# Graph attention over a dense adjacency on one core: the last group of rows is projected beside the first chunk's products

## The chip, the cores and the metric

The kernel runs on one core of a Trainium2 chip. The metric is the device time of one execution in microseconds (us), the median of several runs. Engines: TensorE (PE; PEld its weight loads), VectorE (DVE), ScalarE (ACT), GpSimd (POOL), SyncE (SP, which only issues DMAs here). ACT issues DMAs too.

## The reference, cut to what matters

x is 4096 x 128 float32, adj 4096 x 4096 int32 of zeros and ones (67 MB), W 128 x 128, a 256 x 1.

```python
h = jnp.maximum(_layernorm(x, axis=-1), 0.0)
Wh = h @ W
a1, a2 = (a[:Fout, 0], a[Fout:, 0])
e = (Wh @ a1)[:, None] + (Wh @ a2)[None, :]
e = jnp.where(e > 0, e, ALPHA * e)          # ALPHA = 0.2
e = jnp.where(adj > 0, e, MASK_VAL)
attention = jax.nn.softmax(e, axis=1)
h_prime = attention @ Wh
out = x + jax.nn.elu(h_prime)
```

## The kernel before, in words

**Tiling.** The 4096 output rows are cut into four chunks of 1024 (c = 0 to 3), the 4096 columns of adj into eight units of 512 (u = 0 to 7), each of four tiles of 128 (q = 0 to 3). x is cut into eight blocks b of 512 rows, two of which make a group g of 1024 rows.

**The weights.** The weight of an entry factors: up to a factor per output row it is the larger of two exponentials, one of the output row (g_row, spread over the partitions) and one of the column (gq_word). VectorE makes the words of one tile (c, u, q) in one instruction, L826: max(g_row, gq_word) times the transposed adjacency byte, 128 x 1024. A word is 32 bits that hold the two float16 halves (high and low) of a weight. TensorE multiplies them with the values (Wh times the column's exponential, also as a high and a low float16, `val`): three matmuls of 128x129 for each of eight row tiles, 24 for one product (L1052 to L1054), summed in three PSUM banks `acc[:, 0:3]` over the whole chunk. The fourth bank, `aux`, is free for other things.

**The adjacency.** SP (from load 12 on SP and ACT, half each) loads it as int32 into a ring of four 2 MB slots `raw`. The list LOADS gives the order: an entry is a whole unit (two halves by rows, rows of 2 KB), half the rows of two units (rows of 4 KB), or a quarter of four units for a "set". A slot is asked for again when ACT has made bytes of it (`act_bytes`). ACT turns each half slot to bytes with a Sign of 128x2048 (`to_bytes`, `one_of_two_to_bytes`, `set_to_bytes`; L540, L552, L574). The bytes of a unit are transposed by TensorE (`turn`, 16 transposes, L1028) into `mask_t`, for the last four units of chunks 2 and 3 (the sets) by VectorE (`turn_set`, L806). `words` has four buffers, so VectorE runs up to four products ahead of TensorE (`words_free`).

**The start.** For each group g: VectorE takes statistics (`row_halves`, L741) and moments; ACT and POOL centre the rows (`centre`, L512, L418); TensorE transposes them (`turn_x`, L996) into `mask_t[:, 1]`; ACT rectifies them into `h_t` (L520); TensorE projects them (`project`, L1007) into banks 0 to 2 of acc; VectorE scales them into `wh_sb` (`keep_projected`, L767); ACT takes the exponentials (L528); VectorE makes the column words (`make_words`, `split_weights_sums`, L773 to L786); `spread_words` on TensorE and `row_copy` on ACT make g_row (L1016, L592, L596). Values: the product in float32 (`first_values` on VectorE for group 0, `weigh` L429 on POOL), the cast to float16 on ACT (`high_values`, L535), the rest on VectorE or POOL (`first_low_values` L797, L432). Before the change all four groups are projected before the first product, since they pass through the banks that the products sum into; POOL weighs groups 1 to 3 beside the first units.

**Order.** Each engine's program is written out by hand, in order; semaphores join them. Chunk 0 is special: units' turns, spreads of groups 1 to 3 (units 3 to 5) and the mean of Wh for `seed_row` (unit 6) stand between products. POOL, after its values, sums Wh for the mean; the tails of the chunks (division, elu, residual) run on DVE, POOL and ACT beside later products.

## Time and profile before

| | |
|---|---|
| median of 3 runs | 236.33 us (235.15 to 236.42) |
| profiled execution | 236.24 us, its span 234.5 us |
| PE busy | 219.9 us (94%) |
| DVE busy | 198.9 us (85%) |
| ACT busy | 158.3 us (68%) |
| POOL busy | 81.1 us (35%) |
| mean granted TensorE clock | 0.984 |
| HBM read | 70.32 MB |

Busy time is the union of an engine's instructions, so it says how long an engine had something to do, not that it did it at its peak. The timeline merges neighbouring instructions of one line; its bracket is the idle time of the engine ahead of the row and what ended it. The chain is followed back from the last instruction, at each step to what released it.

### The profile page before, as it was taken

The numbers are of one execution on the slowest core, as the hardware profiler recorded it, in microseconds if no ns is written. First come the engines' busy times: TensorE is split into PE (matmuls) and PEld (weight loads), VectorE is DVE, ScalarE is ACT, GpSimd is POOL, SyncE is SP. The second block draws the span as 40 slices with busy tenths as digits, with TensorE's granted clock in tenths as the row PEclk, the third lists the DMA queues.
The fourth block names the chain that finished last, engine by engine and source line by source line (L and its number), as shares of the span: only waits on it lengthen the run. The fifth ranks groups of instructions, "written<-read, shape, count | busy, mean of one in ns | idle before, by whom it ended". The sixth has DMA issues, their size and how long they took to land.

```text
span 234.5 us, 8071 instructions
## 1 busy us (share of the span) xinstructions
PE 219.9 (94%) x3608; PEld 213.9 (91%) x3608; DVE 198.9 (85%) x266; ACT 158.3 (68%) x139; POOL 81.1 (35%) x68
## 2 busy tenths in 40 slices
PE   5969999999999999999999999999997899999980
PEld 1659899999999999999999999999997899999980
DVE  3999988765687997877787987899999999998766
ACT  3598899997786689874666666686569630991043
POOL 3648118789100031999300200000008900089000
PEclk9997999999999999999999999999999999999996
DMA  6999999999999999999999999999999930402002
GB/s 216 345 392 404 407 408 408 407 408 407 407 408 407 409 402 410 411 402 404 247 319 352 343 325 338 355 365 328 307 405 409 395 120 0 182 3 89 6 0 91
DMA packets 25526, 72.93 MB, mean 311 GB/s; under 512 B 1554, under 2 KB 2068, under 8 KB 25492
## 3 DMA queue, kind: packets, MB, share of 16 engines
q1 hardware_dynamic: 17040, 49.81, 57.3%
q10 hardware_dynamic: 8452, 22.61, 27.0%
q8 instruction: 28, 0.46, 0.9%
q14 instruction: 6, 0.05, 0.1%
HBM read 70.32 MB, written 2.10 MB: 309 GB/s over the span
## 4 chain that ended last, share of the span: by engine, by line
PE 59%; DMA 10%; ACT 10%; DVE 9%; issue 7%; ACTq 4%; DVEq 0%
PE acc L1052 16%; PE acc L1054 16%; PE acc L1053 16%; DMA raw<-in_adj_dram 8%; PE mask_t L1028 8%; ACTq L585 4%; ACT second L574 3%; DVE words L826 2%; ACT mask L552 2%; DVE stats L741 1%; DMA first<-in_x_dram 1%; PE acc L1016 1%; DVE mask_t L806 1%; ACT neg L705 1%; ACT g_row L574 1%
## 5 line engine op out<-in xcount | busy, mean ns | idle before, releaser
L826 DVE SCALAR_TENSOR_TENSOR words<-g_row,gq_word,mask_t 128x1024 f32<-128x1024 f32 x96 | 119.7, 1276 | 25.1 <-PE mask_t L1028 11.9
L1052 PE MATMUL acc<-val,words 128*128 128x129 f16 x744 | 127.9, 220 | 0.3 <-DVE wh_sb L767 0.3
L1054 PE MATMUL acc<-val,words 128*128 128x129 f16 x744 | 127.9, 220 | 0.0
L1053 PE MATMUL acc<-val,words 128*128 128x129 f16 x744 | 127.9, 220 | 0.0
L552 ACT ACTIVATE mask<-raw,step_bias 128x2048 uint8<-128x2048 int32 x44 | 86.0, 1995 | 28.9 <-PE mask_t L1028 14.0
L1052 PEld LDWEIGHTS acc<-val,words 128*128 128x128 f16 x744 | 72.8, 98 | 0.5 <-issue 0.5
L1053 PEld LDWEIGHTS acc<-val,words 128*128 128x128 f16 x744 | 72.8, 98 | 0.1
L1054 PEld LDWEIGHTS acc<-val,words 128*128 128x128 f16 x744 | 72.8, 98 | 0.0
L1052 PE MATMUL acc<-first,words 128*128 128x129 f16 x256 | 44.0, 220 | 2.3 <-DVE words L826 1.5
L1053 PE MATMUL acc<-first,words 128*128 128x129 f16 x256 | 44.0, 220 | 0.0
L1054 PE MATMUL acc<-first,words 128*128 128x129 f16 x256 | 44.0, 220 | 0.0
L826 DVE SCALAR_TENSOR_TENSOR words<-g_row,first,mask_t 128x1024 f32<-128x1024 f32 x32 | 38.7, 1266 | 0.0
L462 POOL TENSOR_SCALAR hp<-hp 128x1024 f32<-128x1024 f32 x3 | 10.9, 3636 | 68.8 <-ACT neg L665 68.8
L1052 PEld LDWEIGHTS acc<-first,words 128*128 128x128 f16 x256 | 25.0, 98 | 3.1 <-DVE words L826 3.0
L1028 PE MATMUL mask_t<-ident_b,mask 128*128 128x128 bf16 x384 | 26.2, 223 | 0.0
L1053 PEld LDWEIGHTS acc<-first,words 128*128 128x128 f16 x256 | 25.1, 98 | 0.0
L1054 PEld LDWEIGHTS acc<-first,words 128*128 128x128 f16 x256 | 25.1, 98 | 0.0
L1028 PEld LDWEIGHTS mask_t<-ident_b,mask 128*128 128x128 bf16 x384 | 23.4, 100 | 0.1
L574 ACT ACTIVATE second<-raw,step_bias 128x2048 uint8<-128x2048 int32 x8 | 15.6, 1996 | 7.6 <-issue 7.6
L458 POOL TENSOR_TENSOR hp<-num,rz 128x1024 f32<-128x1024 f32 x3 | 5.7, 1897 | 42.3 <-DVE rz L837 42.2
L574 ACT ACTIVATE g_row<-raw,step_bias 128x2048 uint8<-128x2048 int32 x4 | 8.0, 2004 | 8.5 <-DMA raw<-in_adj_dram 6.9
L485 POOL COPY first<-val 32x640 uint32<-32x640 uint32 x16 | 11.4, 715 | 1.0
(113 smaller groups left out, 214.9 us busy)
## 6 DMA issues: line engine op xcount, KB each, us to landing
raw<-in_adj_dram SPq DMA_DIRECT2D x36, 1024.0 KB, 15.6
raw<-in_adj_dram ACTq DMA_DIRECT2D x12, 1024.0 KB, 11.6
raw<-in_adj_dram SPq DMA_DIRECT2D x16, 512.0 KB, 11.1
raw<-in_adj_dram ACTq DMA_DIRECT2D x16, 512.0 KB, 13.5
first<-in_x_dram SPq DMA_DIRECT2D x8, 256.0 KB, 6.8
val<-in_x_dram SPq DMA_DIRECT2D x2, 512.0 KB, 15.8
out_dram<-first ACTq DMA_DIRECT2D x2, 512.0 KB, 4.6
out_dram<-val ACTq DMA_DIRECT2D x1, 512.0 KB, 3.8
```

The costliest lines, as they stand in the source:

```text
L458: nc.gpsimd.tensor_tensor(hp[:], num[:, :, 0:F], rz[:].unsqueeze(2).broadcast_to([P, CT, F]), ALU.mult).then_inc(hp_ready, 1)
L462: nc.gpsimd.tensor_scalar(hp[:], hp[:], 0.0, -1.0, ALU.max, ALU.add).then_inc(pos_ready, 1)
L485: nc.gpsimd.tensor_copy(val_set_u[k * QUARTER:(k + 1) * QUARTER, 4 * m:4 * m + 4], val_u[m * QUARTER:(m + 1) * QUARTER, (4 + k) * BT:(5 + ...
L552: nc.scalar.activation(mask[:, mask_slot(c, u), h * BT:(h + 1) * BT], raw_two[at % RING][:, :, i * BLOCK:(i + 1) * BLOCK], ACT.Sign, scale ...
L574: nc.scalar.activation(pair_bytes[PAIRS[c][k]][:, :, h], raw[:, at % RING, :, k * 256:(k + 1) * 256].rearrange("p t (m x) -> p m t x", m=2 ...
L585: act.dma_start(raw[k * QUARTER:(k + 1) * QUARTER, at % RING], adj_set[c, 1, h, k]).then_inc(set_in[at % RING], 16)
L705: last = nc.scalar.activation(neg[:, t], num[:, t, 0:F], ACT.Exp, scale=rz[:, t:t + 1])
L826: nc.vector.scalar_tensor_tensor(words[:, q], g_row[:, c * CHUNK:(c + 1) * CHUNK], word, bytes_t, ALU.max, ALU.mult).then_inc(words_ready, 1)
L1028: last = nc.tensor.transpose(maskt_pairs[:, i % 2, h, t * P:(t + 1) * P], mask_pairs[:, mask_slot(c, u), t, :, h], ident_b[:])
L1052: nc.tensor.matmul(acc_tile(t), high, v[:, 0, 0:V], start=first and t % PT == 0, stop=False, skip_group_check=True)
L1053: nc.tensor.matmul(acc_tile(t), high, v[:, 1, 0:V], start=False, stop=False, skip_group_check=True)
L1054: last = nc.tensor.matmul(acc_tile(t), low, v[:, 0, 0:V], start=False, stop=False, skip_group_check=True)
```

## The change

Group 3's transposes, projection, constants, values and g_row leave the start and go between products of chunk 0 (g_row into chunk 1), through the fourth bank `aux`. TensorE turns unit 0 before it transposes x 4 and 5, and begins with the products when group 2 is kept. VectorE's statistics of blocks 6 and 7 go into units 1 and 2, their moments to (2, 3), behind a new wait for the low values of group 2; its keeps of group 3 go into unit 5, the constants are made for groups 1 and 2 at (1, 1) and for group 3 at (5, 3). Values 1 (the second half of group 0) go from VectorE to POOL. Units 2 and 3 of chunk 0 are loaded and made to bytes as whole units (rows of 2 KB); unit 1 is loaded before x 6 and 7. The row copies on ACT move accordingly, those of group 3 to loads 14 and 16 of chunk 1, and VectorE's seed_row to the end of chunk 0.

The diff; left out are hunks that only move counts of semaphores:

```diff
@@ -51,7 +51,7 @@
-    LOADS = [(0, u, None) for u in range(2)] + [(0, (u, u + 1), k) for u in (2, 4, 6) for k in range(2)]
+    LOADS = [(0, u, None) for u in range(4)] + [(0, (u, u + 1), k) for u in (4, 6) for k in range(2)]
     LOADS += [(1, (u, u + 1), k) for u in (0, 2, 4, 6) for k in range(2)] + [(SETS, (u, u + 1), k) for u in (0, 2) for k in range(2)]
@@ -346,9 +346,11 @@
             load_raw(0, 1)
+            load_raw(1, 0)
+            load_raw(1, 1)
             for b in range(6, NB):
                 load_x(b)
-            for at in range(1, C * U):
+            for at in range(2, C * U):
@@ -418,9 +420,22 @@
+            def first_values(k):
+                tt = slice(k * BT, (k + 1) * BT)
+                pool.wait_ge(z_ready, 1)
+                nc.gpsimd.tensor_tensor(v32[:, 0, tt], wh_sb[:, tt, 0:F], dv[:, tt].unsqueeze(2).broadcast_to([P, BT, F]), ALU.mult
+                                        ).then_inc(v32_first, 1)
+            def first_low_values(k):
+                tt = slice(k * BT, (k + 1) * BT)
+                pool.wait_ge(vh_ready, k + 1)
+                pool.wait_ge(vl_first, k)
+                nc.gpsimd.tensor_tensor(val[:, tt, 1, 0:F], v32[:, 0, tt], val[:, tt, 0, 0:F], ALU.subtract).then_inc(vl_first, 1)
             def weigh(g):
-                pool.wait_ge(z_ready, 2)
+                pool.wait_ge(z_ready, 2 if g < 3 else 3)
@@ -434,12 +449,20 @@
             inverse_deviation(1, BT, CT)
-            for g in range(1, G):
+            def centre_group(g):
                 centre(2 * g)
                 inverse_deviation(g + 1, g * CT, (g + 1) * CT)
-            for g in range(1, G):
-                weigh(g)
+            centre_group(1)
+            first_values(1)
+            centre_group(2)
+            first_low_values(1)
+            weigh(1)
+            weigh(2)
+            centre_group(3)
+            weigh(3)
...
@@ -517,7 +540,7 @@
                     act.wait_ge(wh_ps, 3 * (b // 2 - 2) + 3)
-                nc.scalar.activation(h_t[:, b % 4], turned_bank(b), ACT.Relu, scale=-1.0).then_inc(ht_ready, 1)
+                nc.scalar.activation(h_t[:, b % 4], turned_bank(b) if b < 6 else aux, ACT.Relu, scale=-1.0).then_inc(ht_ready, 1)
@@ -629,36 +652,41 @@
             high_values(0, BT, CT)
+            to_bytes(0, 1, 0)
+            to_bytes(0, 1, 1)
+            exponentials(1, 3)
+            to_bytes(0, 2, 0)
+            to_bytes(0, 2, 1)
+            high_values(1, 0, CT)
+            to_bytes(0, 3, 0)
+            to_bytes(0, 3, 1)
+            high_values(2, 0, CT)
+            two_to_bytes(4)
             centre(6)
             centre(7)
-            to_bytes(0, 1, 0)
+            one_of_two_to_bytes(5, 0)
             rectify(6)
+            one_of_two_to_bytes(5, 1)
             rectify(7)
-            to_bytes(0, 1, 1)
-            exponentials(1, G)
-            two_to_bytes(2)
-            two_to_bytes(3)
-            high_values(1, 0, CT)
-            two_to_bytes(4)
-            high_values(2, 0, CT)
-            two_to_bytes(5)
+            two_to_bytes(6)
+            one_of_two_to_bytes(7, 0)
+            exponentials(3, G)
+            one_of_two_to_bytes(7, 1)
+            row_copy(1, 0)
             high_values(3, 0, CT)
-            row_copy(1, 0)
-            two_to_bytes(6)
+            one_of_two_to_bytes(8, 0)
             row_copy(1, 1)
-            one_of_two_to_bytes(7, 0)
-            row_copy(2, 0)
-            one_of_two_to_bytes(7, 1)
-            row_copy(2, 1)
-            one_of_two_to_bytes(8, 0)
-            row_copy(3, 0)
             one_of_two_to_bytes(8, 1)
             one_of_two_to_bytes(9, 0)
-            row_copy(3, 1)
+            row_copy(2, 0)
             one_of_two_to_bytes(9, 1)
             load_half(9 + RING)
+            one_of_two_to_bytes(10, 0)
+            row_copy(2, 1)
+            one_of_two_to_bytes(10, 1)
+            load_half(10 + RING)
@@ -674,8 +702,11 @@
-            for at in range(U + 2, C * U):
+            for at in range(U + 3, C * U):
                 c, u, h = LOADS[at]
+                if at in (14, 16):
+                    row_copy(3, (at - 14) // 2)
                 if u is None:
@@ -764,7 +795,7 @@
                 dve.wait_ge(rstd_ready, g + 2 if g else 1 + (t1 > BT))
-                nc.vector.tensor_tensor(wh_sb[:, tt], projected(acc[:, k, :], t1 - t0),
+                nc.vector.tensor_tensor(wh_sb[:, tt], projected(acc[:, k, :] if g < 3 else aux, t1 - t0),
                                         half_rstd[:, tt].unsqueeze(2).broadcast_to([P, t1 - t0, W2]), ALU.mult).then_inc(wh_ready, 1)
...
@@ -855,33 +886,38 @@
             first_low_values(0)
-            first_values(1)
             for k in range(3):
                 keep_projected(1, k)
-            row_halves(6)
-            link(row_halves(7))
-            moments(4, 3 * CT, 4 * CT)
-            first_low_values(1)
-            for k in range(3):
-                keep_projected(2, k)
             dve.wait_ge(grow_ready, 2)
             for k in range(3):
-                keep_projected(3, k)
+                keep_projected(2, k)
             weights(0, 0, 2)
             weights(0, 0, 3)
             for u in range(1, U):
                 for q in range(BT):
-                    if (u, q) == (1, 2):
-                        make_words(1, G, 6)
-                        split_weights_sums(1, G, 6)
-                        dve.wait_ge(word_ready, 4)
-                    if (u, q) == (7, 2):
-                        dve.wait_ge(mean_ps, 1)
-                        dve.wait_ge(consts, 6)
-                        nc.vector.tensor_scalar(seed_row[:, 0:F], aux[:, 0:F], SEED / N, None, ALU.mult).then_inc(mean_ready, 1)
+                    if (u, q) == (1, 1):
+                        make_words(1, 3, 6)
+                        split_weights_sums(1, 3, 6)
+                    if (u, q) == (1, 3):
+                        row_halves(6)
+                    if (u, q) == (2, 1):
+                        link(row_halves(7))
+                    if (u, q) == (2, 3):
+                        dve.wait_ge(vl_ready, 2)
+                        moments(4, 3 * CT, 4 * CT)
+                    if u == 5 and q < 3:
+                        keep_projected(3, q)
+                    if (u, q) == (5, 3):
+                        make_words(3, G, 9)
+                        split_weights_sums(3, G, 9)
                     weights(0, u, q)
+            dve.wait_ge(mean_ps, 1)
+            dve.wait_ge(consts, 6)
+            nc.vector.tensor_scalar(seed_row[:, 0:F], aux[:, 0:F], SEED / N, None, ALU.mult).then_inc(mean_ready, 1)
             dve.wait_ge(mean_ready, 1)
@@ -991,25 +1027,30 @@
-                    pe.wait_ge(ht_ready, b - 1)
+                    pe.wait_ge(ht_ready, b - 1 if b < 7 else b)
+                bank = turned_bank(b) if b < 6 else aux
                 for q in range(BT):
-                    last = nc.tensor.transpose(turned_bank(b)[:, q * P:(q + 1) * P], hn[:, b % 2, q], ident[:])
+                    last = nc.tensor.transpose(bank[:, q * P:(q + 1) * P], hn[:, b % 2, q], ident[:])
                 last.then_inc(ht_ps, 1)
                 pe.wait_ge(ht_ready, 2 * g + 1 + (t1 > BT))
-                if g >= 1:
+                if g == 3:
+                    pe.wait_ge(ht_ready, NB)
+                    pe.wait_ge(wh_ready, 3 * g + k)
+                elif g >= 1:
                     pe.wait_ge(wh_ready, 3 * (g - 1) + k + 1)
-                bank = projected(acc[:, k, :], PT)
+                bank = projected(acc[:, k, :] if g < 3 else aux, PT)
                 for t in range(t0, t1):
             def spread_words(g, k):
-                pe.wait_ge(word_ready, 4 if g else 2)
+                pe.wait_ge(word_ready, (2, 4, 4, 6)[g])
                 bank = mask_t[:, 0, k, :] if g == 0 else aux
@@ -1044,7 +1085,7 @@
                         if c == 0:
-                            pe.wait_ge(wh_ready, 3 * (G - 1) + t // PT + 1)
+                            pe.wait_ge(wh_ready, 3 * 2 + t // PT + 1)
                         else:
@@ -1105,18 +1146,14 @@
                 project(1, k)
-            turn_x(4)
-            turn_x(5)
             turn(0, 0)
+            turn_x(4)
+            turn_x(5)
             for k in range(3):
                 project(2, k)
-            turn_x(6)
-            turn_x(7)
-            for k in range(3):
-                project(3, k)
@@ -1124,6 +1161,8 @@
                     pe.wait_ge(z_ready, 2)
+                if u == 6:
+                    pe.wait_ge(z_ready, 3)
                 if u < 2:
@@ -1132,18 +1171,25 @@
                     product(0, u, q)
-                    if q == 1 and u < U - 1:
+                    if q == (1 if u else 2) and u < U - 1:
                         if u == 0:
-                            pe.wait_ge(ht_ready, NB)
+                            pe.wait_ge(ht_ready, 6)
                         turn(0, u + 1)
-                    if u in (3, 4, 5) and q % 2 == 0:
-                        i = 2 * (u - 3) + q // 2
-                        if i >= 1:
+                    if u == 3 and q % 2 == 0:
+                        turn_x(6 + q // 2)
+                    if u == 4 and q < 3:
+                        project(3, q)
+                    if u in (5, 6) and q % 2 == 0:
+                        i = 2 * (u - 5) + q // 2
+                        if i == 0:
+                            pe.wait_ge(wh_ready, 3 * G)
+                        else:
                             pe.wait_ge(grow_ready, 2 + i)
                         spread_words(1 + i // 2, i % 2)
-                    if (u, q) == (6, 3):
-                        pe.wait_ge(grow_ready, 2 * G)
+                    if (u, q) == (7, 2):
+                        pe.wait_ge(grow_ready, 6)
                         pe.wait_ge(wh_sum, G + 2)
@@ -1159,6 +1205,13 @@
                             product(c, u, q)
+                            if c == 1 and u in (1, 2) and q == 1:
+                                if u == 1:
+                                    pe.wait_ge(mean_ready, 1)
+                                else:
+                                    pe.wait_ge(grow_ready, 7)
+                                spread_words(3, u - 1)
                             if late and q == 1:
```

## Rows read from the trace of the kernel before

**Rows 1.** The page's slices of the span, 40 slices of 5.9 us: tenths busy, GB/s

```profile
PE 219.9 (94%) x3608; PEld 213.9 (91%) x3608; DVE 198.9 (85%) x266; ACT 158.3 (68%) x139; POOL 81.1 (35%) x68
...
DMA  6999999999999999999999999999999930402002
...
GB/s 216 345 392 404 407 408 408 407 408 407 407 408 407 409 402 410 411 402 404 247 319 352 343 325 338 355 365 328 307 405 409 395 120 0 182 3 89 6 0 91
```

**Rows 2.** The chain that ended last, merged: start us, length us, what; two turns, one unit apart

```profile
80.79 0.89 PE mask_t L1028 x16
...
87.12 0.89 PE mask_t L1028 x16
```

**Rows 3.** Timeline of DVE, late: start us, length us, engine, line, operation, count [idle before <-releaser]

```profile
151.14 1.26 DVE L806 STREAM_TRANSPOSE mask_t<-second 128x1024 uint32<-128x1024 uint32 x1 [0.73 <-ACT second L574]
...
175.91 1.25 DVE L806 STREAM_TRANSPOSE mask_t<-g_row 128x1024 uint32<-128x1024 uint32 x1
```

**Rows 4.** Timeline of ACT, late, columns as in group 3

```profile
119.80 2.00 ACT L552 ACTIVATE mask<-raw,step_bias 128x2048 uint8<-128x2048 int32 x1 [0.75 <-PE mask_t L1028]
...
171.28 2.01 ACT L574 ACTIVATE g_row<-raw,step_bias 128x2048 uint8<-128x2048 int32 x1 [3.99 <-DMA raw<-in_adj_dram]
```

**Rows 5.** Busy time by windows, 4 us: A:B length, PE PEld DVE ACT POOL, PEclk, DMA share, GB/s

```profile
16.00:20.00 4.00, 2.06 (x15) 1.83 (x15) 3.96 (x13) 3.44 (x7) 3.96 (x5) 0.83 1.06 393
```

**Rows 6.** Timeline of PE before and at the first product

```profile
17.94 1.65 PE L996 MATMUL mask_t<-ident,first 128*128 128x128 f32 x8 [1.94 <-ACT first L512]
...
19.39 1.91 PE L1028 MATMUL mask_t<-ident_b,mask 128*128 128x128 bf16 x16
...
21.10 2.47 PE L1007 MATMUL acc<-w_sb,second 128*128 128x130 f32 x16
...
24.69 2.05 PE L1007 MATMUL acc<-w_sb,second 128*128 128x130 f32 x16 [0.25 <-ACT second L520]
...
27.05 0.22 PE L1052 MATMUL acc<-val,words 128*128 128x129 f16 x1 [0.31 <-DVE wh_sb L767]
```

**Rows 7.** Busy time by windows, 0.5 us, columns as in group 5: the granted TensorE clock

```profile
18.50:19.00 0.50, 0.50 (x4) 0.47 (x4) 0.50 (x2) 0.36 (x1) 0.50 (x1) 0.63 1.07 393
...
22.00:22.50 0.50, 0.50 (x6) 0.50 (x5) 0.34 (x2) 0.50 (x2) 0.50 (x1) 0.96 0.99 393
```

**Rows 8.** Timeline of DVE, early

```profile
17.77 1.35 DVE L767 TENSOR_TENSOR wh_sb<-acc,half_rstd 128x390 f32<-128x390 f32 x3
...
19.05 1.63 DVE L741 BATCH_NORM_STATS2 stats<-first 128x6 f32<-128x128 f32 x8
...
23.97 2.46 DVE L826 SCALAR_TENSOR_TENSOR words<-g_row,gq_word,mask_t 128x1024 f32<-128x1024 f32 x2
...
33.26 0.18 DVE L773 TENSOR_SCALAR gq_hi<-gq 128x48 uint32<-128x48 uint32 x1
```

**Rows 9.** Timeline of ACT, early and at its first own load

```profile
17.20 1.27 ACT L512 ACTIVATE first<-first,twice 128x128 f32<-128x128 f32 x4
...
19.64 0.60 ACT L520 ACTIVATE second<-mask_t 128x512 f32<-128x512 f32 x1 [0.40 <-PE mask_t L996]
...
36.23 1.05 ACT L535 CAST val<-second 128x1024 f16<-128x1024 f32 x1
...
37.61 3.90 ACT L552 ACTIVATE mask<-raw,step_bias 128x2048 uint8<-128x2048 int32 x2 [0.34 <-DMA raw<-in_adj_dram]
...
64.99 0.47 ACTq L587 DMA_DIRECT2D raw<-in_adj_dram  x1
```

**Rows 10.** Timeline of POOL, early

```profile
9.69 1.45 POOL L418 TENSOR_SCALAR first<-first,twice 128x128 f32<-128x128 f32 x4 [1.18 <-DVE twice L747]
...
15.91 2.45 POOL L418 TENSOR_SCALAR first<-first,twice 128x128 f32<-128x128 f32 x4 [3.17 <-DVE twice L747]
...
34.29 1.90 POOL L429 TENSOR_TENSOR second<-wh_sb,dv 128x1024 f32<-128x1024 f32 x1 [9.78 <-DVE val L783]
...
37.35 2.16 POOL L432 TENSOR_TENSOR val<-second,val 128x1024 f16<-128x1024 f32 x1 [1.16 <-ACT val L535]
```

4 lines of the change are left out of this document (2 added, 2 removed).

## The prediction, made blind

> **What bounds the kernel now.** I read the page's slices first, then the chain that ended last, then the timelines of the engines where the chain changes engine. The profiled execution took 236.24 us, a span of 234.5 us and 1.74 us around it; the median of the runs shown is 236.33 us, 0.09 us above it. All sums are made against 236.24.
>
> TensorE is busy for 94% of the span, and the DMA engines are full from the second slice to the thirty-second [rows 1]. These two limits take turns. From the first product at 27.05 us [rows 6] TensorE runs without a gap: turns of neighbouring units stand 6.33 us apart, of which 0.89 us is the turn, so one product of 24 matmuls takes (6.33 - 0.89) / 4 = 1.36 us [rows 2]. VectorE needs 1.2 us for the words of one product [rows 8] and follows. From 151 us on it is otherwise: the set units cost VectorE a stream transpose each, and the first of them waits 0.73 us for ScalarE's bytes [rows 3]. From there VectorE is busy without a pause, and TensorE waits for it. ScalarE, for its part, was last released by a TensorE turn at 119.80 us after 0.75 us of waiting [rows 4], and runs from there with its signs and DMA issues back to back. So a TensorE that is late at 119.80 us makes ScalarE late, then VectorE, then the end, one for one.
>
> A TensorE that is early doesn't gain one for one. ScalarE waits 3.99 us for a load that lands at 171.28 us [rows 4]. It makes two signs of 2.0 us from it, so the bytes are there at about 175.2 us, and VectorE takes them at 175.91 us [rows 3]. The slack is 0.7 us. The DMA engines are full up to that point, so the landing doesn't move because somebody asks earlier. **A gain beyond 0.7 us stops there.**
>
> **The change part by part.**
>
> *Start of the products.* Between 16.0 us and 27.05 us TensorE waits 1.94 us for ScalarE's centring, turns x 4 and 5, turns unit 0, projects group 2, turns x 6 and 7, projects group 3 [rows 6]. A projection of a group costs 2.05 us at the full clock, eight transposes of x half of that by their number of matmuls, 1.0 us (an estimate), a unit's turn 0.89 us. Full-speed work is 2 x 2.05 + 2 x 1.0 + 0.9 = 7.0 us in 11.05 us: 4.05 us are lost to waits and to the clock. The granted clock is at half speed (1.2 of 2.4 GHz) from about 18.7 us to 22.0 us [rows 7], after the idle stretch; the turn of unit 0 shows it, 1.91 us for what costs 0.9 later [rows 6].
>
> After the change TensorE turns unit 0 first. Its second bytes are made just before ScalarE's centring starts at 17.20 us [rows 9], so the turn can go at 17.4 us and ends at 18.3. Then x 4 and 5 (19.4), ScalarE's two rectifications of 0.6 us [rows 9], project group 2 from 19.6 to 21.6. VectorE no longer makes values 1, statistics 6 and 7 or their moments here: its keep of group 1 (1.35 us for three, [rows 8]) ends at 18.5, words 0 and 1 at 20.9, keep of group 2 follows the projection. First product at 21.6 us, after 5.6 us with 3.95 us of work: 1.65 us lost instead of 4.05. **Gain 2.4 us.** This supposes that the clock stays up, since the wait shrinks from 1.94 to about 1.4 us. If it falls as before, the stretch from 18.7 us on costs 1.3 us more and the gain is 1.1. I take the full clock and keep the other end.
>
> *Group 3 inside the chunk.* Its transposes (1.0), its projection (2.05) and the mean move behind products; two of six spreads move on into chunk 1. All of it is TensorE work at the same price, so it moves and costs nothing by itself. What it costs is in the waits.
>
> *VectorE's load in units 1 and 2.* It gets statistics 6 and 7 (1.63 us for both, [rows 8]), the moments (0.9 us), a keep of three (1.35 us, unit 5), and its words' constants twice instead of once (six small operations from 33.26 us on, 0.9 us, [rows 8]). With words 1.2 us against products of 1.36 us it has 0.6 us to spare in a unit, and 1.5 with a turn. At (1,1) it makes the constants after the first words of unit 1, and words (1,1) come about 0.65 us after TensorE wants them. **Stall 0.65.**
>
> *The new wait for the second low values, at (2,3).* Queued behind it on VectorE are the moments of group 3, words (2,3) and all later words; TensorE waits for those, and POOL and ScalarE wait for the moments before they centre x 6 and 7. POOL: constants at 28.6 us, weigh 1 with 1.9 us, ScalarE's cast 1.05, subtraction 2.16, then again for group 2 [rows 9, 10], with ScalarE's signs of units 2 and 3 between: 28.6 + 1.9 + 1.05 + 2.15 = 33.7; 33.7 + 1.9 + 1.05 + 2.15 = 38.8 us. Moments until 39.7, words (2,3) until 40.95. TensorE wants them at 40.05. **Stall 0.9.** This row has no counterpart before; its bounds are 0 (loads and casts early) and 2.8 us (the sign of unit 3 waits for its load as the one at 37.61 us did, [rows 9]).
>
> *Later waits of unit 3 to 7.* Worked out in the same way, the projection's bank handed back by VectorE (0.45 us each, one product between), the row copies, values 3 (wanted at 65.2 us, ready at 64.6) and the mean come in time. The thinnest is values 3, with 0.6 us.
>
> *The loads.* ScalarE waits some 2 us for group 3 in unit 5, so it gives raw slot 0 back at 67.0 us and not at 64.99 [rows 9]. Requests for 4 us of DMA are still queued then; no cost. Units 2 and 3 of chunk 0 come as whole units, in rows of 2 KB and not 4 KB. While 2 KB rows are in flight the engines move 393 GB/s [rows 5], later 408 [rows 1]: 4.19 MB cost 10.66 us and not 10.27, so everything behind them lands 0.4 us later. At 171.28 us this takes 0.4 of the slack of 0.7.
>
> *Sum.* TensorE reaches chunk 1 2.4 - 0.65 - 0.9 = 0.85 us ahead. VectorE would reach 175.91 us 0.85 earlier, and meets the bytes at 175.2 + 0.4 = 175.6: 0.3 us gained. **236.24 - 0.3 = 235.9 us**, with 0 and 0.85 us (no late landing) as its near ends.
>
> A rule of the Trainium skill speaks against one part. POOL's four centring operations take 1.45 us in one place and 2.45 us in another, where VectorE runs arithmetic between two tensors [rows 10]. The page SBUF — State Buffer, section "Who interferes with whom", says that VectorE and GpSimd share a port pair under an exclusive lock; the change gives POOL values 1 and puts its chain in front of VectorE's wait. By the rows POOL's chain could be up to 1.0 us late; by the rule this happens only where VectorE has two SBUF operands, and the words take theirs partly from PSUM, so the sum stays.
>
> **The rivals.**
>
> *Slower: VectorE's wait at (2,3) becomes the bound.* POOL, ScalarE and VectorE form one chain through values 1 and 2, and every microsecond that it is late beyond 39.65 us (38.8 plus the lead of 0.85) is lost at the end. For it: ScalarE is full in this stretch, and a clock that falls as before shifts TensorE's first product and with it the whole chain by 1.3 us; a POOL chain 1.0 us late comes on top. With the clock alone: 1.3 - 0.85 = 0.45 us slower, 236.7. With both, or with a load of unit 3 as late as that at 37.61 us (stall 2.8 and not 0.9), 1.45 to 1.9 us slower: 237.7 to 238.1. Against it: units 2 and 3 are asked for early, and their first halves landed in time before.
>
> *Faster: the landing at 171.28 us isn't fixed.* The rate in the slices from 112 to 175 us goes between 247 and 365 GB/s with the engines full [rows 1], so it depends on which loads are together. If earlier releases mix them better, the whole lead counts: 235.4; with the two stalls absent as well, 0.85 + 1.55 = 2.4 us: 233.8. I put this case at 234.8, its middle. Against it: nothing shows that an earlier request speeds a full engine.
>
> *It doesn't do what it says: TensorE starts 5 us earlier and loses all of it again* in stalls of units 1 to 6, level with before, 236.2. This lies in the same band as the forecast.
>
> **How the numbers follow.** The forecast and its neighbours (lead used up by the landing, clock fallen without further delay, all lost again), 235.1 to 237.4: 0.46. Faster rival: 0.29. Slower rival beyond the band: 0.25. About 0.5%, 1.2 us, is what a measurement of this kernel can tell from no change, so these are the three chances. The predicted time is 235.9. The range reaches from 234.3 (the faster rival without its last stall) to 238.0 (the slower rival nearly in full).
>
> **What would show it.** First product at 21 to 23 us in the timeline of PE, and the granted clock between 18 and 22 us; VectorE idle before the moments of group 3, released by POOL, with TensorE idle by about 1 us behind it; the last product of chunk 0 at about 79 us and not 80.8; the wait of the first set transpose (0.73 us before); the landing of the load before 171.28, and whether VectorE now waits at 175.6. The prediction is wrong if that landing moves by more than 0.5 us either way, if TensorE's lead at the end of chunk 0 isn't between -0.5 and 2.4 us, or if ScalarE's late release of raw slots leaves the DMA engines idle anywhere between 60 and 90 us.

## The result, and the profile after

The changed kernel took 239.56 us (median of 8 runs, 237.61 to 240.59) beside 236.38 us of the kernel before on the same chip: a ratio of 1.0131, with a 95% interval of 1.0095 to 1.0167. It is slower by 1.3%; 235.9 us had been forecast, with a range up to 238.0. Ratios, here and below, leave out single runs that lie more than 1.5% above the fastest run of their kernel (one each of e1_seed_late, e5_no_wait and e7_seed_late_half). The profiled execution took 239.97 us with a span of 238.2 us, 3.73 us more than the profiled one before.

The start came nearly as forecast. TensorE's timeline (start us, length us, engine, line, operation, count, idle before and releaser) answers to [rows 6]:

```profile
17.93 1.05 PE L1069 MATMUL mask_t<-ident_b,mask 128*128 128x128 bf16 x16 [1.98 <-ACT mask L563]
18.82 1.04 PE L1033 MATMUL mask_t<-ident,first 128*128 128x128 f32 x8
20.11 2.05 PE L1048 MATMUL acc<-w_sb,second 128*128 128x130 f32 x16 [0.25 <-ACT second L543]
22.20 0.22 PE L1093 MATMUL acc<-val,words 128*128 128x129 f16 x1
```

The first product stands at 22.20 us, 4.85 us ahead of the 27.05 before. But TensorE still waits 1.98 us, now for the bytes of unit 0. The new wait of VectorE at (2,3) is there too, and TensorE's idle time behind it; the timelines of DVE and PE:

```profile
39.91 0.17 DVE L778 TENSOR_TENSOR twice<-stats 128x8 f32<-128x8 f32 x1 [1.61 <-POOL val L447]
```

```profile
42.17 0.23 PE L1093 MATMUL acc<-val,words 128*128 128x129 f16 x1 [1.21 <-DVE words L857]
```

The loss is elsewhere, at the seam of chunks 0 and 1. VectorE's timeline there:

```profile
70.55 4.86 DVE L857 SCALAR_TENSOR_TENSOR words<-g_row,gq_word,mask_t 128x1024 f32<-128x1024 f32 x4 [2.36 <-PE mask_t L1069]
78.95 0.29 DVE L920 TENSOR_SCALAR seed_row<-acc 128x128 f32<-128x128 f32 x1 [3.55 <-PE acc L1194]
79.28 3.66 DVE L857 SCALAR_TENSOR_TENSOR words<-g_row,gq_word,mask_t 128x1024 f32<-128x1024 f32 x3
82.86 1.35 DVE L865 TENSOR_TENSOR num<-acc,seed_row 128x387 f32<-128x387 f32 x3
```

VectorE has all words of chunk 0 done at 75.4 us and then idles 3.55 us for one small operation, the scaling of `seed_row`, which needs TensorE's mean. In the kernel before that operation stood ahead of the last two tiles' words and waited 0.52 us for an earlier mean:

```profile
74.49 0.29 DVE L883 TENSOR_SCALAR seed_row<-acc 128x128 f32<-128x128 f32 x1 [0.52 <-PE acc L1148]
```

Behind the wait stand the first three tiles' words of chunk 1 (3.66 us) and then `take_sums`, which frees the banks that TensorE's first product of chunk 1 writes. TensorE turns the next unit and stops. First its rows, then busy time by windows (A:B, length, then busy us of PE, PEld, DVE, ACT, POOL, then the granted clock, DMA share, GB/s):

```profile
78.48 0.44 PE L1194 MATMUL acc<-second,ones 128*128 128x128 f32 x2
...
83.56 0.22 PE L1093 MATMUL acc<-val,words 128*128 128x129 f16 x1 [2.39 <-DVE num L865]
```

```profile
80.00:84.00 4.00, 1.61 (x29) 1.46 (x27) 4.00 (x6) 2.83 (x3) 0.00 (x0) 1.00 1.02 408
84.00:88.00 4.00, 4.00 (x46) 4.00 (x43) 2.85 (x4) 3.44 (x2) 1.90 (x1) 0.57 1.04 414
88.00:92.00 4.00, 4.00 (x75) 4.00 (x73) 3.73 (x3) 3.33 (x2) 0.00 (x0) 1.00 1.01 402
```

TensorE's pause is 2.39 us by its bracket. After it the granted clock is near its half level (1.2 of 2.4 GHz): 46 matmuls are counted between 84 and 88 us and 75 in the next 4 us. From the first product (83.56 us) to the turn of unit 2 (90.63 us) this takes 7.07 us; in e2_before_seed_end below, with the same pause and the clock at 1.00, it takes 5.44 us. The clock costs 1.63 us, and the two together 4.0 us. In chunk 1 the turn of unit 2 shows where both kernels stand; before and after:

```profile
86.96 1.06 PE L1028 MATMUL mask_t<-ident_b,mask 128*128 128x128 bf16 x16
```

```profile
90.63 1.06 PE L1069 MATMUL mask_t<-ident_b,mask 128*128 128x128 bf16 x16
```

3.67 us later, and 3.73 us later at the end. That the two nearly agree is chance. Two spreads of group 3 are still owed behind this turn (0.89 us), so the turn of unit 4 comes at 104.17 us and not at 99.62, 4.55 us later. Of these 0.81 us are given back at 151 us: there the kernel before has VectorE wait 0.73 us for ScalarE's bytes [rows 3], and here it doesn't. The late load of [rows 4] lands at 170.22 us. In neither kernel does VectorE wait for its bytes: the kernel before takes them at 175.91 us, 0.7 us behind ScalarE's signs. The page shows the seam too, in its slices of the span (tenths of the granted clock): the 7 in the fifteenth slice (83 to 89 us) is the seam, and the 7 that the kernel before had in its fourth slice is gone.

```profile
PEclk9999999999999979999999999999999999999997
```

Of the eight runs two had a mean granted clock of 0.992 and 0.993 and took 237.92 and 237.61 us; the six at 0.985 or 0.986 took 239.27 to 240.59. So a fall of the clock at the seam, with some 2 us, probably came in those six and not in the two; only the profiled run shows where its clock fell.

### The profile page after: what moved, and what is told of

Its sections match the earlier page's. It is cut to its first block, busy times and chain, and to the rows that moved or that the text cites. A ratio compares the mean times of both kernels' runs of the same rounds, so it can differ in the third digit from the quotient of the medians.

```text
span 238.2 us, 8079 instructions
## 1 busy us (share of the span) xinstructions
PE 220.5 (93%) x3608; PEld 214.1 (90%) x3608; DVE 198.4 (83%) x270; ACT 158.8 (67%) x142; POOL 82.3 (35%) x70
## 4 chain that ended last, share of the span: by engine, by line
PE 66%; DVE 17%; DMA 5%; issue 4%; POOL 3%; ACT 3%; SPq 1%; POOLq 0%; DVEq 0%
PE acc L1093 18%; PE acc L1094 18%; PE acc L1095 18%; DVE words L857 12%; PE mask_t L1069 8%; DMA raw<-in_adj_dram 5%; DVE mask_t L837 2%; POOL val L447 2%; PE acc L1048 2%; POOL second L444 2%; SPq L325 1%; PE acc L1057 1%; ACT neg L736 1%; ACT mask L563 1%; ACT second L733 1%
## 5 line engine op out<-in xcount | busy, mean ns | idle before, releaser
L1093 PE MATMUL acc<-val,words 128*128 128x129 f16 x744 | 129.9, 221 | 3.6 <-DVE num L865 2.4
L1094 PE MATMUL acc<-val,words 128*128 128x129 f16 x744 | 129.9, 221 | 0.5 <-issue 0.5
L1095 PE MATMUL acc<-val,words 128*128 128x129 f16 x744 | 129.9, 221 | 0.0
L575 ACT ACTIVATE mask<-raw,step_bias 128x2048 uint8<-128x2048 int32 x40 | 78.7, 1997 | 33.5 <-PE mask_t L1069 21.2
L1069 PE MATMUL mask_t<-ident_b,mask 128*128 128x128 bf16 x384 | 25.4, 219 | 2.0 <-ACT mask L563 2.0
L1069 PEld LDWEIGHTS mask_t<-ident_b,mask 128*128 128x128 bf16 x384 | 22.4, 98 | 2.1 <-issue 2.1
L563 ACT ACTIVATE mask<-raw,step_bias 128x2048 uint8<-128x2048 int32 x7 | 13.8, 2000 | 1.0 <-DMA raw<-in_adj_dram 1.0
L444 POOL TENSOR_TENSOR second<-wh_sb,dv 128x1024 f32<-128x1024 f32 x3 | 5.7, 1904 | 24.6 <-DVE val L814 24.6
```

The source lines that it names most:

```text
L444: nc.gpsimd.tensor_tensor(v32[:, g % 2], wh_sb[:, group(g), 0:F], dv[:, group(g)].unsqueeze(2).broadcast_to([P, CT, F]), ALU.mult).then_in ...
L563: nc.scalar.activation(mask[:, mask_slot(c, u), k * BT:(k + 1) * BT], raw[:, at % RING, k * BT:(k + 1) * BT], ACT.Sign, scale=1.0, bias=st ...
L575: nc.scalar.activation(mask[:, mask_slot(c, u), h * BT:(h + 1) * BT], raw_two[at % RING][:, :, i * BLOCK:(i + 1) * BLOCK], ACT.Sign, scale ...
L1069: last = nc.tensor.transpose(maskt_pairs[:, i % 2, h, t * P:(t + 1) * P], mask_pairs[:, mask_slot(c, u), t, :, h], ident_b[:])
L1093: nc.tensor.matmul(acc_tile(t), high, v[:, 0, 0:V], start=first and t % PT == 0, stop=False, skip_group_check=True)
L1094: nc.tensor.matmul(acc_tile(t), high, v[:, 1, 0:V], start=False, stop=False, skip_group_check=True)
```

## The experiments

Two explanations were set against each other first. The seam (theory S of the texts below): the loss is the place of one wait, VectorE's `seed_row` at the end of chunk 0, with the clock's fall behind it. The others: it is in the loads (2 KB rows, slots given back later) or in the new wait at (2,3). Ratios are to the kernel before on the same chip, where it took 235.41 us (e1 to e4), 235.57 (e5 to e8), 235.74 (e9 to e11) and 235.66 us (e12) in the median; a ratio isn't exactly the quotient of two medians. The first four expectations count in microseconds from the 236.4 us of the first chip, so there the ratios are what to compare.

| kernel | ratio (95%) | median us | runs |
|---|---|---|---|
| after | 1.0131 (1.0095 to 1.0167) | 239.56 | 8 |
| e1_seed_late | 1.0041 (1.0014 to 1.0068) | 236.23 | 12 |
| e2_before_seed_end | 1.0142 (1.0104 to 1.0180) | 238.54 | 4 |
| e3_after_awake | 1.0108 (1.0072 to 1.0144) | 238.37 | 4 |
| e4_before_whole_units | 0.9989 (0.9967 to 1.0011) | 235.27 | 12 |
| e5_no_wait | 1.0037 (1.0007 to 1.0067) | 236.68 | 12 |
| e6_before_half | 0.9985 (0.9953 to 1.0018) | 235.39 | 10 |
| e7_seed_late_half | 1.0001 (0.9977 to 1.0025) | 235.34 | 10 |
| e8_no_wait_half | 0.9983 (0.9967 to 0.9999) | 235.13 | 12 |
| e9_raw_first | 1.0049 (1.0021 to 1.0077) | 237.08 | 12 |
| e10_before_raw_first | 1.0013 (0.9990 to 1.0036) | 236.24 | 10 |
| e11_x_first | 1.0078 (1.0052 to 1.0104) | 237.80 | 8 |
| e12_seed_late_held | 1.0044 (1.0015 to 1.0073) | 236.54 | 12 |

**The wait put behind the words (e1_seed_late).** The changed kernel, with the scaling of `seed_row` moved from the end of chunk 0 to just ahead of `take_sums`, behind three tiles' words:

```diff
-            dve.wait_ge(mean_ps, 1)
-            dve.wait_ge(consts, 6)
-            nc.vector.tensor_scalar(seed_row[:, 0:F], ...).then_inc(mean_ready, 1)
-            dve.wait_ge(mean_ready, 1)
...
+                            if c == 1:
+                                dve.wait_ge(mean_ps, 1)
+                                dve.wait_ge(consts, 6)
+                                nc.vector.tensor_scalar(seed_row[:, 0:F], ...).then_inc(mean_ready, 1)
+                                dve.wait_ge(mean_ready, 1)
                             take_sums(c - 1)
```

> The changed kernel with one edit: VectorE scales the mean into seed_row just before it takes the sums of chunk 0 (after three words of chunk 1), not at the end of chunk 0. Theory S (VectorE blocked 3.55 us behind the mean, TensorE therefore idle 2.39 us at 81 us, and 1.6 us more because the granted clock falls to half from 84 to 88 us): both go, 4.0 us back, about 235.6 us median, and TensorE's clock stays at 1.00 between 80 and 90 us. Rival C (the fall of the clock has another cause than this idle stretch): 2.4 us back, 237.2 us. Rival D (the loads bound the end from 110 us on, the stall at 81 us is paid for by them anyway): less than 1 us back, 238.6 us or more.

Measured: 0.9 of the 1.3% come back, 2.1 us and not the 4.0 expected. VectorE's 3.55 us of idle time are gone, and so is TensorE's pause:

```profile
79.15 0.28 DVE L934 TENSOR_SCALAR seed_row<-acc 128x128 f32<-128x128 f32 x1
79.46 1.36 DVE L865 TENSOR_TENSOR num<-acc,seed_row 128x387 f32<-128x387 f32 x3
```

From the turn of unit 1 to that of unit 2 in chunk 1 TensorE takes 6.34 us here (79.38 to 85.72 us) and 10.52 in the changed kernel (80.11 to 90.63): the seam cost 4.18 us in that profile. The rest of what should have come back is lost later. The profiled execution took 235.99 us. That this is near the forecast of 235.9 says little, since the kernel before took 235.41 us on this chip. It shows the forecast's cap. VectorE comes early to the set transpose and waits for bytes whose load landed at 171.59 us; the rows of ACT and DVE, beside 171.28 [rows 4] and 175.91 [rows 3] before:

```profile
171.59 2.00 ACT L597 ACTIVATE g_row<-raw,step_bias 128x2048 uint8<-128x2048 int32 x1 [4.69 <-DMA raw<-in_adj_dram]
```

```profile
175.58 1.26 DVE L837 STREAM_TRANSPOSE mask_t<-g_row 128x1024 uint32<-128x1024 uint32 x1 [0.77 <-issue]
```

That wait is put down to "issue", but it ends where ScalarE's two signs of 2.0 us behind the landing end (171.59 + 3.9 = 175.5). So S holds for most of the loss, and 0.4% stays open.

**The same wait in the kernel before (e2_before_seed_end).** There the mean is moved behind product (7,2) and the scaling to the chunk's end, and nothing else:

```diff
-                    if (u, q) == (7, 2):
-                        dve.wait_ge(mean_ps, 1)
-                        dve.wait_ge(consts, 6)
-                        nc.vector.tensor_scalar(seed_row[:, 0:F], ...).then_inc(mean_ready, 1)
                     weights(0, u, q)
+            dve.wait_ge(mean_ps, 1)
+            dve.wait_ge(consts, 6)
+            nc.vector.tensor_scalar(seed_row[:, 0:F], ...).then_inc(mean_ready, 1)
             dve.wait_ge(mean_ready, 1)
...
-                    if (u, q) == (6, 3):
+                    if (u, q) == (7, 2):
                         pe.wait_ge(grow_ready, 2 * G)
```

> The kernel before with that one part of the change alone: TensorE's mean goes from after product (6,3) to after product (7,2), VectorE's seed_row to the end of chunk 0. Theory S: VectorE waits some 3.5 us there, TensorE idles 2 to 2.5 us at the start of chunk 1, and the clock falls: 236.4 + 3.5 to 4.0 = 240 to 240.4 us. Rival D: within 1 us of before, 236.4 to 237.4 us. If only the idle stretch counts and the clock stays: 238.8 us.

Measured 1.0142: one moved wait makes the kernel before as slow as the changed one. The pause of TensorE is the same to the hundredth:

```profile
83.52 0.22 PE L1051 MATMUL acc<-val,words 128*128 128x129 f16 x1 [2.39 <-DVE num L834]
...
88.96 1.06 PE L1027 MATMUL mask_t<-ident_b,mask 128*128 128x128 bf16 x16
```

In this profile the clock stayed at 1.00 from 84 to 88 us, the turn of unit 2 comes 5.44 us behind the first product (7.07 in the changed kernel), and the run (237.49 us) was the fastest of its four; the others, at 0.985 to 0.988, took 238.23 to 239.69. As a ratio 1.015 to 1.017 had been expected with the fall of the clock and 1.010 without it; the measured interval reaches from one to the other.

**The clock alone (e3_after_awake).** The changed kernel, with nine matmuls of 512 columns that nobody reads, behind `mean_ready` and ahead of the first product of chunk 1, to keep TensorE busy in the pause:

```diff
+                        if (c, u) == (1, 0):
+                            pe.wait_ge(mean_ready, 1)
+                            for _ in range(9):
+                                nc.tensor.matmul(aux, ident_b[:], ident_b[:].unsqueeze(1).broadcast_to([P, BT, P]), start=True, stop=True)
```

> The changed kernel with nine added matmuls of 512 columns into the free fourth bank, before the first product of chunk 1 and behind the seed_row: TensorE still can't go on, but isn't idle for long. Theory S: the clock stays up and 1.6 us come back, 238.0 us, with the start of product (1,0,0) unchanged at about 83.5 us. Rival C: the clock falls as well, 239.6 us. Rival D: 239.6 us too, but with the clock up.

Measured 238.37 us, a ratio of 1.0108 for 1.0131; the granted clock was 0.993 to 0.997 in all four runs. With intervals of 1.0072 to 1.0144 and 1.0095 to 1.0167 the run times don't show that anything came back, and 1.6 us (0.7%) had been expected. What shows the clock's share is the traces. Here the turn of unit 2 comes 5.44 us behind the first product (82.84 to 88.28 us), as in e2_before_seed_end. The cover is seen, and the clock that stays:

```profile
80.29 2.11 PE L1209 MATMUL acc<-ident_b 128*128 128x512 bf16 x9
```

```profile
84.00:88.00 4.00, 4.00 (x75) 4.00 (x73) 4.00 (x4) 3.18 (x3) 1.71 (x1) 1.00 1.03 407
```

The profiled run (239.61) was the slowest of the four, with a pause of TensorE that nothing in the trace releases, of a sort that comes back below:

```profile
122.05 0.22 PE L1094 MATMUL acc<-val,words 128*128 128x129 f16 x1 [1.52 <-issue]
```

**The size of the rows (e4_before_whole_units).** The kernel before with units 2 and 3 loaded whole, in 2 KB rows:

```diff
-    LOADS = [(0, u, None) for u in range(2)] + [(0, (u, u + 1), k) for u in (2, 4, 6) for k in range(2)]
+    LOADS = [(0, u, None) for u in range(4)] + [(0, (u, u + 1), k) for u in (4, 6) for k in range(2)]
```

> The kernel before with units 2 and 3 of chunk 0 loaded and made to bytes as whole units in rows of 2 KB (SP's order else unchanged). The prediction's term: the DMA engines run at 386 to 394 GB/s for some 10 us longer, every later load lands 0.4 us later, which the slack of 0.7 us takes: 236.4 to 236.8 us. If the loads bound the end more closely than that, up to 237.5 us.

Measured 0.9989: no cost. The rate from 12 to 32 us falls about as forecast, from 402 to 390 GB/s, but the late load still lands at 170.68 us. The size of the rows isn't the cause.

**The wait at (2,3) (e5_no_wait).** e1_seed_late without `dve.wait_ge(vl_ready, 2)` ahead of the moments of group 3.

> e1_seed_late without VectorE's wait for the low values of group 2 ahead of the moments at (2,3), the wait that the prediction priced at 0.9 us of TensorE (measured 1.21). Theory L (the leads of TensorE are capped by the load that lands at about 171 us): TensorE's stall at 41.4 us goes, it is 1.2 us further ahead in chunk 1, and the time doesn't move: within 0.5 us of e1_seed_late (ratio to before about 1.004), with VectorE waiting 1.5 to 2 us for the bytes at 175 us and not 0.77. Rival W (TensorE's lead still counts at the end): 0.8 to 1.2 us faster than e1_seed_late, 235.0 us or less, ratio below 1.000.

Measured 1.0037, no different from e1_seed_late's 1.0041. Taking the wait away doesn't take the delay away. DVE's and POOL's timelines:

```profile
37.61 1.69 DVE L778 TENSOR_TENSOR twice<-stats 128x8 f32<-128x8 f32 x1
39.22 0.16 DVE L779 TENSOR_TENSOR apart<-stats 128x8 f32<-128x8 f32 x1
```

```profile
37.13 2.14 POOL L447 TENSOR_TENSOR val<-second,val 128x1024 f16<-128x1024 f32 x1 [1.16 <-ACT val L558]
```

An operation of 0.17 us takes 1.69 us and ends when POOL's subtraction ends (37.13 + 2.14 = 39.27). TensorE's idle time goes only from 1.21 to 1.04 us. So POOL's values set this point, with or without the wait. The Trainium skill, page SBUF — State Buffer, section "Who interferes with whom", has the rule for it: VectorE and GpSimd share a port pair under an exclusive lock; the trace agrees, with 1.69 us for 0.17.

**The landing at 171 us (e6_before_half, e7_seed_late_half, e8_no_wait_half).** The kernel before, e1_seed_late and e5_no_wait with only half of each set's load brought in, so that part of the sets' weights is made of old bytes; every other instruction stays:

```diff
-  sp.dma_start(raw[..., at % RING], adj_set[c, 1, h, k]).then_inc(set_in[at % RING], 16)
+  sp.dma_start(raw[..., at % RING, 0:BT], adj_set[c, 1, h, k][:, 0:BT]).then_inc(set_in[at % RING], 16)
```

(and the same on ACT's queue).

In these texts and the next ones the letters L and W are new: L says that the landing at 171 us caps TensorE's lead, W that it doesn't.

> The kernel before with half of each quarter of the set loads (eight loads of 2 MB bring 1 MB; the other rows keep old bytes, so the weights of the sets are partly wrong): no engine has less to do, only the DMA engines. Theory L: the load behind 171 us lands some 15 us earlier, VectorE no longer meets it, but in this kernel the meeting was only touched (0.73 us of slack): 235.0 to 235.6 us, ratio 0.997 to 1.000. If the loads cost more than that at the end of before: 234 us.

> e1_seed_late with the same half set loads (weights of the sets partly wrong). Theory L: what kept it from being faster than before was the landing, so now its lead of 0.4 to 0.9 us shows: 0.4 to 0.9 us faster than e6_before_half, about 234.6 us. Rival W: still 0.5 to 1 us slower than e6_before_half.

> e5_no_wait with the same half set loads (weights of the sets partly wrong). Theory L: with the landing gone the missing wait pays in full: 1.2 us faster than e7_seed_late_half, about 233.4 us. Rival W: level with e7_seed_late_half, if ScalarE's chain of signs and DMA issues from 107 us on holds VectorE whatever TensorE does.

With the loads halved the changed kernel stands level with the kernel before (1.0001 and 0.9983 beside 0.9985). It isn't faster: e7_seed_late_half had been expected 0.4 to 0.9 us below e6_before_half, and e8_no_wait_half 1.2 us below that. The edit takes away more than the late landing: ScalarE's pairs of DMA issues also get shorter (0.86 us for 1.48 in most places). What this says of the end is best read from a mark: the words on VectorE near 102 us that wait 1.04 us for TensorE, after both late spreads. Kernel before, and e7_seed_late_half:

```profile
102.15 3.93 DVE L826 SCALAR_TENSOR_TENSOR words<-g_row,gq_word,mask_t 128x1024 f32<-128x1024 f32 x3 [1.04 <-PE acc L1054]
```

```profile
103.31 2.57 DVE L857 SCALAR_TENSOR_TENSOR words<-g_row,gq_word,mask_t 128x1024 f32<-128x1024 f32 x2 [1.04 <-PE acc L1096]
```

| kernel | first turn of TensorE near 18 us | mark | span | span - mark |
|---|---|---|---|---|
| before | 17.94 | 102.15 | 234.5 | 132.35 |
| e4_before_whole_units | 17.91 | 101.58 | 234.2 | 132.6 |
| e1_seed_late | 17.21 | 101.78 | 234.1 | 132.3 |
| e6_before_half | 17.83 | 102.03 | 233.5 | 131.5 |
| e7_seed_late_half | 18.73 | 103.31 | 234.8 | 131.5 |
| e8_no_wait_half | 18.52 | 103.81 | 235.3 | 131.5 |
| e9_raw_first | 17.40 | 102.00 | 233.5 | 131.5 |
| e12_seed_late_held | 17.92 | 103.44 | 234.9 | 131.5 |
| after | 17.93 | 106.69 | 238.2 | 131.5 |

In five variants and the changed kernel itself the end comes 131.5 us after the mark; in e2_before_seed_end, e10_before_raw_first and e11_x_first too (131.45, 131.6 and 131.7 us). Three rows are longer, by 0.8 to 1.1 us, and not all for the same reason. In e1_seed_late it is the landing: VectorE takes the first set transpose 48.2 us after the mark, as e6_before_half does, and waits at 175.58 us. In the kernel before and in e4_before_whole_units it isn't. Both take that first transpose 0.81 and 1.12 us late, after waits of 0.73 and 1.04 us for ScalarE's bytes, and nothing is lost behind it. DVE in the kernel before, [rows 3], against e6_before_half:

```profile
150.21 1.25 DVE L806 STREAM_TRANSPOSE mask_t<-second 128x1024 uint32<-128x1024 uint32 x1
```

What made ScalarE late is in its own timeline: a pair of DMA issues took 2.56 us in the kernel before (2.48 in e4_before_whole_units) where it took 1.49 in e9_raw_first. First the kernel before, then e9_raw_first:

```profile
127.90 2.56 ACTq L585 DMA_DIRECT2D raw<-in_adj_dram  x2
```

```profile
127.72 1.49 ACTq L608 DMA_DIRECT2D raw<-in_adj_dram  x2
```

So the forecast's cap is shown in e1_seed_late, and a second one stands beside it at 151 us. Where the mark is at 103.3 us or later, neither is met. Why the issues take longer in some runs isn't shown.

The table also shows what is left of the lead. Of the changed kernels the three with a granted clock of 1.00 at the start and no further edit, e1, e7 and e9, have their mark 84.57, 84.58 and 84.60 us after the first turn. Nothing in between absorbs a late start, and taking the wait at (2,3) away gains nothing (84.55 us in e5_no_wait). And that first turn, which hangs on unit 0's bytes, stands anywhere from 17.20 us (e3_after_awake) to 18.73, while the six profiles in which x 4 and 5 are turned first (before, e2, e4, e6, e10, e11) all have theirs between 17.83 and 17.98. In e7 the bytes' second half lands late:

```profile
16.58 2.00 ACT L563 ACTIVATE mask<-raw,step_bias 128x2048 uint8<-128x2048 int32 x1 [1.25 <-DMA raw<-in_adj_dram]
```

**Unit 0's bytes asked for earlier (e9_raw_first, e10_before_raw_first).** In e1_seed_late and in the kernel before, the load of the second half of unit 0 put ahead of x 4 and 5 on SP:

```diff
             load_raw(0, 0)
+            load_raw(0, 1)
             for b in range(4, 6):
                 load_x(b)
-            load_raw(0, 1)
```

> e1_seed_late with the second half of unit 0 asked for ahead of x 4 and 5. Theory T (what is left of e1_seed_late against before is the landing of that half: TensorE's first turn now hangs on it directly, and in six traces of the changed order ScalarE began its sign between 15.05 and 16.58 us, always at the landing beyond 15.1): the sign always begins at about 15.1 us, TensorE's first product at 21.5 us, times stay between 235.0 and 236.2 us, median 235.4, ratio to before 0.998 to 1.001. Rival U (the rest comes from later, the landing at 171 us and pauses without a releaser): as e1_seed_late, ratio 1.004, times up to 237.8 us. If x 4 and 5 come too late instead, VectorE's statistics wait at 13.9 us and all of it moves by that.

> The kernel before with the same exchange of loads. Theory T: no change, ratio 0.998 to 1.002, since there the first turn comes 2 us behind the bytes anyway. If x 4 and 5 become late: up to 1 us slower.

The profiled run of e9 did what was wanted: no wait for the bytes, first turn at 17.40, 235.32 us. Its median didn't: 237.08 us, with runs from 235.09 to 238.27, a ratio of 1.0049, no better than e1_seed_late's 1.0041. So theory T fails: the bytes' landing at the start explains where the first turns stand in the profiles, but it isn't what keeps the kernel slower. e10 lost 1.00 us in its profiled run to another pause without a releaser, in the middle of the turn of x:

```profile
19.71 1.09 PE L996 MATMUL mask_t<-ident,first 128*128 128x128 f32 x4 [1.00 <-issue]
```

**The order at the start (e11_x_first).** e1_seed_late with x 4 and 5 turned ahead of unit 0, as before the change:

```diff
+            turn_x(4)
+            turn_x(5)
             pe.wait_ge(grow_ready, 2)
...
             turn(0, 0)
-            turn_x(4)
-            turn_x(5)
```

> e1_seed_late with TensorE's order at the start as before (x 4 and 5 turned first, then unit 0). Theory T: the landing of unit 0's second half no longer matters, but TensorE waits 1.9 us for the centring and its clock falls to half in some runs from 18.7 to 22 us: first product at 22.5 to 23.5 us, 1 to 1.5 us later than in e1_seed_late at its best, a median of 236.3 to 236.8 us with less spread. Rival U: the start doesn't matter within a microsecond, since the landing at 171 us takes it: 236.2 us as e1_seed_late.

Measured 1.0078 (237.80 us, above the 236.3 to 236.8 expected), beside 1.0049 of e9_raw_first on the same chip and 1.0041 of e1_seed_late. The new order seems to be worth 0.3 to 0.4%, though the intervals overlap. TensorE waits 2.05 us and the granted clock falls here, as before the change; group 2's projection takes 3.09 us for 2.05, and the first product stands at 23.83 us:

```profile
20.41 3.09 PE L1049 MATMUL acc<-w_sb,second 128*128 128x130 f32 x16
```

**The lead taken away (e12_seed_late_held).** e1_seed_late with five matmuls of 512 columns ahead of the first product of chunk 1, as the nine of e3_after_awake.

> The kernel e1_seed_late with five matmuls of 512 columns put in front of the first product of chunk 1, which hold TensorE busy for some 1.2 us (nine of them took 2.11 us) and so take away the lead of 1.24 us (turn of unit 2 in chunk 1 at 85.72 us in e1_seed_late, 86.96 us before); it should come at 86.9 to 87.1 us here. All the rest is as in e1_seed_late, whose median stood 0.4% over the kernel before and whose times spread from 235.4 to 239.9 us. Theory L: the lead itself does the harm, since an earlier TensorE asks for the loads of the sets earlier and in another mixture with the other queue, so that the landing at 171 us comes late in some runs. Then this kernel, in step with the kernel before, has its time and its spread: ratio 0.998 to 1.002, seldom a run over 237 us. Rival O: what remains hangs on the orders of ScalarE and SyncE (slots given back later in chunk 0, loads asked in another order) and not on TensorE's phase. Then the spread stays, and the median is that of e1_seed_late or up to 0.8 us more, since the lead no longer covers anything: ratio 1.004 to 1.008, several runs over 237 us.

Measured 1.0044. The turn of unit 2 came at 87.37 and not at 86.9 to 87.1, since this run's first turn was late too (17.92). The size was also chosen badly: 0.89 us of spreads are still owed behind that turn, so the true lead of e1_seed_late was 0.35 us and 1.24 us was too much. In the profile its mark is 1.3 us behind that of the kernel before, less the 0.81 us that VectorE no longer loses at 151 us: 0.5 us by this sum, 0.4 by the spans. No run was faster than 236.08 us, eight of twelve lie within 0.64 us, and four are still over 237, beside three of the seventeen of the kernel before. The theory that the lead itself does the harm had expected 0.998 to 1.002, and is not borne out.

## Why the prediction was wrong, point by point

*What bounds the kernel, and the cap.* Right in part. A TensorE that is late isn't late one for one at the end: 4.54 us at the mark became 3.73, because the 0.81 us that VectorE loses at 151 us in the kernel before go first. That loss, visible as 0.73 us in [rows 3], was also the first thing that an earlier or quicker chain would win. It was read only as the place where ScalarE's lateness enters. The cap at the landing near 171 us is there: e1_seed_late's profile loses its gain on it.

*Start of the products, gain 2.4 us.* Right to 0.6 us: first product at 22.20 and not 21.6, since unit 0's second half of bytes began at 15.79 us in that run (15.05 in e1_seed_late). The clock stayed up, but not for the reason given: the idle time didn't shrink in this run (1.98 us for 1.94), only in e1_seed_late and others (1.45, with 1.4 forecast).

*Stalls at (1,1) and (2,3).* The second is 1.21 us for 0.9, with POOL's values at 39.9 us and not 38.8. At (1,1) the trace lists no wait for words; TensorE instead pauses 0.54 us ahead of 28.45 us, inside the last product of unit 0 and without a releaser, and after that is late enough to find the words nearly made. Taken together with the start, e1_seed_late's mark leads by 0.37 us and not by 0.85.

*The rule on the shared ports.* It was weighed at the wrong place. "The sum stays" was right for the words. But the moments that stand behind the wait begin with operations between two tensors, and e5_no_wait shows one of them held for 1.5 us. What looked like the price of the wait was the price of POOL's work, with or without the wait.

*"Later waits ... and the mean come in time."* **This is the step that failed.** It was asked whether the mean comes in time for the end of the chunk, and it does, as TensorE sees it: 78.48 us, 1.6 us ahead of the end of its last product (80.11 us). It was not asked who waits for it and with what behind. VectorE runs ahead of TensorE and had reached its wait at 75.4 us; behind it in order stood 3.66 us of words and `take_sums`, which TensorE needs. The prediction had named exactly this for the wait at (2,3) and left it out here, a moved step like any other in the diff. Price: 2.39 us of pause and 1.63 us of clock in the profiled run, 4.0 us for a term put at nothing. Against e1_seed_late, where the wait stands behind the words, the seam costs 4.18 us. With this term, and with the lead of 0.85 us counted in full since a late kernel doesn't meet the landing, the forecast is 236.24 - 0.85 + 4.0 = 239.4 us; the profiled run took 239.97. The traces give the difference of the two spans: 4.18 for the seam, less the lead of 0.37 us, plus 0.72 for a first turn at 17.93 and not 17.21 us, less the 0.81 us at 151 us, is 3.72 us for 3.73 measured.

*The loads.* The rate fell, and it cost no time (e4_before_whole_units). That everything behind lands 0.4 us later isn't seen: the late load landed at 170.22 us in the changed kernel, 1.06 us earlier and not 0.4 later, and at 169.74 to 174.70 us in its variants. By the forecast's own sign, a landing moved by more than 0.5 us, this part was wrong; it was treated as fixed and scatters by several microseconds.

*The rivals.* The slower one put the loss in VectorE's wait at (2,3), with up to 1.9 us. The side was right, the mechanism (a wait of VectorE in front of TensorE's work) was of the same kind, the place was wrong. The middle of the faster rival's 233.8 and 235.4 us is 234.6 and not 234.8, which changes nothing.

*What stays open.* With the failed step mended the kernel is still 0.4 to 0.5% slower by the ratios (e1_seed_late, e5_no_wait, e9_raw_first, e12_seed_late_held), although the best runs of the first three took 235.40, 234.93 and 235.09 us. The start may be a part of it: its lead of 0.37 us is smaller than the scatter of the first turn, and the old order didn't have that scatter. What is plain is a tail. Over 237 us came 20 of the 48 runs of e1, e5, e9 and e12, 3 of the 22 of e7 and e8, and 4 of 100 of the kernel before beside them (2 of 8 in the first measurement). The one profile from the tail's end, e5_no_wait's 240.29 us, has a wait of VectorE at 151 us (1.16 us, ScalarE's issues again at 2.51), a late landing, a second wait of VectorE (2.54 us), a pause of TensorE of 3.47 us, and again half the clock. It is one run and doesn't speak for the other 19; its rows of ACT and PE and its windows:

```profile
174.70 2.00 ACT L597 ACTIVATE g_row<-raw,step_bias 128x2048 uint8<-128x2048 int32 x1 [4.16 <-DMA raw<-in_adj_dram]
```

```profile
181.88 0.27 PE L1093 MATMUL acc<-first,words 128*128 128x129 f16 x1 [3.47 <-DVE num L865]
```

```profile
180.00:184.00 4.00, 2.12 (x20) 2.15 (x21) 3.97 (x7) 3.97 (x4) 3.63 (x1) 0.60 1.01 400
184.00:188.00 4.00, 4.00 (x42) 4.00 (x41) 4.00 (x4) 4.00 (x3) 3.92 (x2) 0.54 1.01 406
```

Whether late landings make the tail, and why it is longer in these kernels, isn't shown: the wait at (2,3), the place of unit 0's load and the lead were each taken away, and none took the tail along. Only with the sets' loads halved were the tail shorter and the 0.4% gone. That points to these loads, by their landing or by ScalarE's issuing of them, which no run separates. No version with whole loads beats the kernel before.

## What to carry to other kernels

A step that moves in one engine's program moves a wait in another's. For each moved step ask which engine waits for its result, when that engine gets there (one that runs ahead gets there early), and what stands behind the wait in its order; put such a wait behind the work that doesn't need it. A start gained is worth only what the next late transfer leaves of it, so read the slack at the last wait for a load first; and where a pause of some 2 us appears on TensorE, count with the clock as a second price that may or may not come (1.63 us here).
